# Sorted finish per tile, a split first load, and batch 0's norm and expert choice in the last scan step

## What is computed

```
h = einsum('bhid,oi,od->bho', x, weighted_sum, weight)
x = layernorm(h)
for _ in range(4):
    x = mamba_block(simple_rmsnorm(x), ...)   # in: conv (4 taps), silu, B, C, delta; 16 states per channel; out
h = h + x
z = layernorm(h)
expert = argmax(z @ W_router)                 # one of 4 for each token
y = gelu(z @ W1[expert] + b1[expert]) @ Wo + bo + z
h = h + layernorm(y) * gamma + beta
```

## Time and profile before

| | us |
|---|---|
| median of 3 runs (1889.51 to 1893.72) | 1891.31 |
| profiled execution | 1891.32 |
| its span, first to last instruction | 1889.2 |
| TensorE busy | 1782.5 (94%) |
| VectorE busy | 1552.8 (82%) |
| ScalarE busy | 1543.8 (82%) |
| GpSimd busy | 1510.4 (80%) |

### The profile page before, as it was taken

One profiled execution on the slowest core, in us unless ns is written; L12 is line 12 of the kernel. 1 busy time (PEld: TensorE's weight loads), 2 busy tenths in 40 slices (PEclk: granted clock), 3 DMA queues, 4 the chain that ended last, 5 costly groups with the idle time before them and its releaser, 6 DMA issues.

```text
span 1889.2 us, 31478 instructions
## 1 busy us (share of the span) xinstructions
PE 1782.5 (94%) x11920; PEld 1415.4 (75%) x11920; DVE 1552.8 (82%) x1707; ACT 1543.8 (82%) x2579; POOL 1510.4 (80%) x874
## 2 busy tenths in 40 slices
PE   6989899999999999999999999999999988789993
PEld 3447687878787878787878787878788777789993
DVE  1368989898989898989898989898989989853243
ACT  0269999999999999999999999999999987832230
POOL 0029999999999999999999999999999987631422
PEclk9999999999999999999999999999999989899997
DMA  7211111121212121211111111111111211163641
GB/s 272 99 68 45 58 47 68 44 71 40 74 38 76 37 71 44 71 44 67 48 62 52 59 56 57 58 54 61 50 65 46 80 57 68 38 250 129 231 143 59
DMA packets 46392, 144.24 MB, mean 76 GB/s; under 512 B 7009, under 2 KB 18529, under 8 KB 42914
## 3 DMA queue, kind: packets, MB, share of 16 engines
q1 hardware_dynamic: 41538, 114.97, 17.5%
q0 software_dynamic: 4704, 27.27, 4.0%
HBM read 119.67 MB, written 22.54 MB: 75 GB/s over the span
## 4 chain that ended last, share of the span: by engine, by line
PE 41%; ACT 24%; POOL 20%; DVE 8%; issue 6%; DMA 1%; SPq 0%; POOLq 0%; DVEq 0%; ACTq 0%
POOL hid L524 13%; ACT hid L709 12%; ACT dub_t L724 9%; PE b_ps L1469 8%; PE y_all L1482 7%; DVE hid L1141 6%; PE bank_a L1601 4%; POOL dub_t L515 4%; PE bank_b L1337 3%; PE y_all L1222 3%; PE bank_a L1337 2%; POOL du L505 2%; PE b_ps L1585 2%; PE y_all L1585 2%; PE bank_a L1346 2%
## 5 line engine op out<-in xcount | busy, mean ns | idle before, releaser
L1141 DVE TENSOR_TENSOR_SCAN hid<-hid,b_ps 128x512 f32<-128x512 f32 x1024 | 1199.2, 1206 | 102.0 <-PE b_ps L1469 89.6
L524 POOL TENSOR_TENSOR hid<-hid,c_rep 128x1024 f32<-128x1024 f32 x506 | 1191.8, 2390 | 97.7 <-DVE hid L1141 97.4
L1469 PEld LDWEIGHTS b_ps<-ident,dub_t 128*128 128x128 f32 x4096 | 486.4, 142 | 300.2 <-issue 180.5
L1469 PE MATMUL b_ps<-ident,dub_t 128*128 128x128 f32 x4096 | 630.7, 277 | 42.7 <-DVE hid L1141 40.4
L709 ACT ACTIVATE hid<-delta,neg_a 128x512 f32<-128x512 f32 x1024 | 659.6, 714 | 0.2
L1482 PE MATMUL y_all<-ident,hid 128*128 128x128 f32 x4096 | 620.5, 275 | 0.0
L724 ACT ACTIVATE dub_t<-du_t,b_t 128x512 f32<-128x512 f32 x784 | 505.2, 714 | 30.0 <-PE b_ps L1469 29.6
L1482 PEld LDWEIGHTS y_all<-ident,hid 128*128 128x128 f32 x4096 | 484.1, 142 | 2.9 <-POOL hid L524 2.7
L515 POOL TENSOR_SCALAR dub_t<-du_t,b_t 128x512 f32<-128x512 f32 x240 | 162.4, 702 | 0.0
L934 DVE SCALAR_TENSOR_TENSOR u<-bank_b,conv_w_sb,u 128x511 f32<-128x511 f32 (+2 forms) x192 | 139.6, 727 | 0.7
L1316 PE MATMUL bank_b<-xn,w_in_sb 128*128 128x512 f32 x256 | 129.9, 603 | 5.4 <-DVE u L934 3.9
(11 more groups left out here) (211 smaller groups left out, 1593.7 us busy)
## 6 DMA issues: line engine op xcount, KB each, us to landing
c_rep<-bc_dram SPq DMA_DIRECT2D x128, 512.0 KB, 3.7
hid<-x_t SPq DMA_DIRECT2D x4, 2048.0 KB, 8.5
xt<-x_dram SPq DMA_DIRECT2D x15, 512.0 KB, 3.4
x_dram<-x_out SPq DMA_DIRECT2D x15, 512.0 KB, 2.9
z_dram<-du SPq DMA_DIRECT2D x2, 1408.0 KB, 19.2
y_dram<-hid SPq DMA_DIRECT2D x22, 128.0 KB, 2.1
h_dram<-hid SPq DMA_DIRECT2D x4, 512.0 KB, 4.3
x_dram<-hid SPq DMA_DIRECT2D x3, 512.0 KB, 2.7
```

Of the source, the lines that this page charges most:

```text
L524: nc.gpsimd.tensor_tensor(part, part, c_rep[:, n % 2, s % GROUP, :].unsqueeze(1) .broadcast_to([P, HALF, SEQ]), ALU.mult).then_inc(hc_read ...
L1141: nc.vector.tensor_tensor_scan(hid[:, i % RING, d, :], hid[:, i % RING, d, :], b_ps[d % 2][:, :], 0.0, ALU.mult, ALU.add)\
L1469: last = nc.tensor.transpose(b_ps[d % 2][:, c * P:(c + 1) * P], dub_t[:, i % DUB, c, d * P:(d + 1) * P], ident[:, :])
```

## The change

It has four parts.

**Start.** The loads of `wd` and of batch 0's `x_t`, now in two halves, are issued from ScalarE's queue beside SyncE's; `wc` is made in two halves, and the token product waits for each half. The zeros for `z_dram` are no longer written at the start: `clear_rows` writes those of one pair in step 4 and of the other in step 6, together with zeros for `h2_dram` and padding ids for `id_dram`.

**Head of batches 0 and 1.** Epsilon and the scaling are GpSimd's (`head_root`); the statistics are spread over several slots. Batch 0's root and scaling move from step 14 to (15, 0), its turns to (15, 1) and (15, 2), the logits to (15, 3), the choice to (15, 4). `choose` reads the scores from PSUM and has seven instructions.

**Finish.** `h2` (the residual) and the token ids are scattered in the order of the tiles, as z is, and loaded back; z and h2 of a tile lie side by side in `z_part`. Each tile is then finished in its sorted order: `add_y` (y from PSUM plus z plus bias), `tile_moments`, `tail_root`, `tile_finish`, and an indirect transfer from GpSimd puts each row at its token's place in `out`, which has 22 x 128 more rows for the padding. `y_dram`, its stores and the gathers are gone. From tile 6 on the projections alternate between two banks.

**Order.** `rank(1)` and `lay_out(1)` come one tile earlier, `last_out` and the logits of batch 2 and 3 stand behind a projection instead of ahead of it.

```
+LATE = {6: (0, 1), 7: (2, 3), 8: (4,), 9: (5,), 10: (6,), 11: (7,), 12: (8, 9), 13: (10, 11)}
+FINISH_AT = [LATE.get(t, (t - 2,) if t > 13 else ()) for t in range(ALL_TILES)]
+MOMENTS_OF = [() if t in (0, LAY_T) else (t - 2, t - 1) if t == LAY_T + 1 else (t - 1,) for t in range(ALL_TILES)]
+ROOTS_AT = [{0: (), 1: (), 2: (0, 1), 5: (), 6: (4, 5)}.get(t, (t - 1,)) for t in range(ALL_TILES)]
...
+                    act.dma_start(hid[:, 0, :, :], x_t[0, :, 0:NI, :]).then_inc(x_first, 16)
+                    for d in range(TAPD):
+                        act.dma_start(wd[d::TAPD, :], w_t[d, :].partition_broadcast(P // TAPD)).then_inc(tw_in, 16)
+                    act.dma_start(hid[:, 1, :, :], x_t[0, :, NI:2 * NI, :]).then_inc(xT_in[0], 16)
...
+                    def clear_rows(g):
+                        sp.wait_ge(zero_made, 1)
+                        for rows, done in ((z_dram[g], z_zeroed), (h2_dram[g], h2_zeroed)):
+                            sp.dma_start(rows.rearrange("(j p) o -> p j o", p=P),
+                                         zero[:, :].unsqueeze(1).broadcast_to([P, TILES, D])).then_inc(done, 16)
+                        sp.wait_ge(ids_made, 2)
+                        sp.dma_start(id_dram[g].rearrange("(j p) o -> p j o", p=P),
+                                     pad_id[:, g * TILES:(g + 1) * TILES].unsqueeze(2), allow_slow_non_contiguous=True).then_inc(id_set, 16)
...
+                            if k in (4, 6) and g == 5:
+                                clear_rows((k - 4) // 2)
...
                     load_z(0)
                     store_x(STEPS - 2)
                     load_x_tokens(2)
-                    for p in range(3):
-                        store_y(p)
+                    load_h2(0)
+                    load_ids(0)
                     load_z(1)
...
+                    load_h2(1)
+                    load_ids(1)
...
                     def head_root(b):
+                        pool.wait_ge(bn_ready, 2 * TC * (b + 1))
+                        own = 2 if b == BATCH - 1 else 0
+                        nc.gpsimd.tensor_scalar(f_norm[:, own, :], moments[:, own, :, 1], 1e-5, None, ALU.add).then_inc(f_ve_ready, 1)
                         pool.wait_ge(f_ve_ready, b + 1)
-                        own = 2 if b == BATCH - 1 else 0
                         nc.gpsimd.tensor_tensor(f_norm[:, own, :], f_norm[:, own, :], half_power[:, :], ALU.pow).then_inc(f_root_ready, 1)
...
+                        for c in range(TC):
+                            nc.gpsimd.tensor_scalar(f_z[b][:, c, :], f_h2[b][:, c, :], moments[:, own, c, 0:1], f_norm[:, own, c:c + 1],
+                                                    ALU.subtract, ALU.mult).then_inc(z_ready, 1)
...
-                                if (k, s, half) == (STEPS - 2, 11, 1):
+                                if (k, s, half) == (STEPS - 1, 0, 1):
                                     head_root(0)
...
+                    for t in range(ALL_TILES):
+                        if t + WBUF < ALL_TILES:
+                            load_w1(t + WBUF)
...
+                        for n in ROOTS_AT[t]:
+                            tail_root(n)
...
+                        for n in FINISH_AT[t]:
+                            send_out(n)
+                    send_out(ALL_TILES - 2)
+                    tail_root(ALL_TILES - 1)
+                    send_out(ALL_TILES - 1)
...
-                    Z_T_COPY_AT = {(STEPS - 2, 15): (0, 0), (STEPS - 1, 0): (0, 1), (STEPS - 1, 9): (1, 1)}
+                    Z_T_COPY_AT = {(STEPS - 1, 1): (0, 0), (STEPS - 1, 2): (0, 1), (STEPS - 1, 9): (1, 1)}
...
+                        tt(o_row[:, t % O_RING, :], out_ps(t), z_rows(t)[:, 0:D], ALU.add).then_inc(y_added, 1)
...
-                    MOMENTS_AT = {(STEPS - 2, 11, 0): 0, (STEPS - 1, 5, 3): 1}
-                    SCALE_AT = {(STEPS - 2, 13, 0): 0, (STEPS - 1, 7, 0): 1}
-                    CHOOSE_AT = {(STEPS - 1, 2, 1): 0, (STEPS - 1, 9, 3): 1}
+                    STATS_AT = {(STEPS - 2, 10, 0): (0, 0), (STEPS - 2, 10, 1): (0, 1), (STEPS - 2, 11, 0): (0, 2), (STEPS - 2, 11, 1): (0, 3),
+                                (STEPS - 1, 4, 3): (1, 0), (STEPS - 1, 5, 0): (1, 1), (STEPS - 1, 5, 3): (1, 2), (STEPS - 1, 6, 0): (1, 3)}
+                    MEAN_AT = {(STEPS - 2, 11, 2): 0, (STEPS - 1, 6, 1): 1}
+                    CHOOSE_AT = {(STEPS - 1, 4, 0): 0, (STEPS - 1, 9, 3): 1}
...
-                            pe.wait_ge(y_kept, TURN_OF[t])
+                            pe.wait_ge(y_added, t - 1)
...
-                    Z_TURN_AT = {(STEPS - 2, 14, 0): (0, 0), (STEPS - 2, 15, 3): (0, 1), (STEPS - 1, 7, 3): (1, 0), (STEPS - 1, 8, 1): (1, 1)}
-                    LOGITS_AT = {(STEPS - 1, 0, 3): 0, (STEPS - 1, 9, 2): 1}
+                    Z_TURN_AT = {(STEPS - 1, 1, 2): (0, 0), (STEPS - 1, 2, 2): (0, 1), (STEPS - 1, 7, 3): (1, 0), (STEPS - 1, 8, 1): (1, 1)}
+                    LOGITS_AT = {(STEPS - 1, 3, 2): 0, (STEPS - 1, 9, 2): 1}
```

More of the change, by code:

```diff
@@ L298, in logits_ps, with out_ps, z_rows @@
                 return (bank_b[:, :] if b < 2 else y_ps[DC + b - 2])[:, 0:TC * EXPERTS]
+            def out_ps(t):
+                return (y_ps[DC + 1] if t >= BANKED and t % 2 else bank_a)[:, 0:D]
+            def z_rows(t):
+                return z_part[t // TILES][t % TILES // 4][:, t % TILES % 4, :]
             def rank_ps(g):
@@ L417, in store_out, with load_h2 @@
-                    def store_out(b):
-                        sp.wait_ge(res_ready, b + 1)
-                        sp.dma_start(out[b], y_tok[b]).then_inc(res_stored, 16)
+                            sp.dma_start(z_part[g][i][:, 0:n, 0:D], rows[:, 4 * i:4 * i + n, :]).then_inc(z_in[g][i], 16)
+                    def load_h2(g):
+                        sp.wait_ge(h2_out[g], 16 * CH)
+                        rows = h2_dram[g].rearrange("(j p) o -> p j o", p=P)
+                        for i in range(3):
+                            n = min(4, TILES - 4 * i)
+                            sp.dma_start(z_part[g][i][:, 0:n, D:2 * D], rows[:, 4 * i:4 * i + n, :]).then_inc(h2_in[g], 16)
@@ L901, in _ @@
                     dve.wait_ge(tw_in, 2 * TAPD * 16)
-                    nc.vector.tensor_tensor(wc, ws, wd.unsqueeze(1).broadcast_to([P, KT, D]), ALU.mult).then_inc(wc_ready, 1)
+                    for half in range(2):
+                        rows = slice(half * NI, (half + 1) * NI)
+                        nc.vector.tensor_tensor(wc[:, rows, :], ws[:, rows, :], wd.unsqueeze(1).broadcast_to([P, NI, D]), ALU.mult)\
+                            .then_inc(wc_ready, 1)
                     center(0)
@@ new lines, in tile_finish @@
+                    def tile_finish(t):
+                        o = t % O_RING
+                        dve.wait_ge(t_root_ready, t + 1)
+                        dve.wait_ge(centered, t + 1)
+                        if t % TILES == 0:
+                            dve.wait_ge(h2_in[t // TILES], 3 * 16)
+                        nc.vector.scalar_tensor_tensor(o_row[:, o, :], o_row[:, o, :], tile_norm[:, o:o + 1], z_rows(t)[:, D:2 * D],
+                                                       ALU.mult, ALU.add).then_inc(res_ready, 1)
```

395 lines of the change are left out of this document (208 added, 187 removed).

## The result

The changed kernel takes 1870.21 us (median of 4 runs, 1869.42 to 1873.22), the kernel before beside it 1892.37 us; the ratio is 0.9893 [0.988, 0.9905]. Forecast were 1854 us: 22 us came of the 37.7.

What follows compares the result with a forecast made beforehand. Four engines 94 to 99% busy bound inner steps, TensorE the tiles; 29.1 us without matmul followed. Terms -23.4 - 0.6 - 6.5 - 4.5 - 3.7 + 1.0 = -37.7 took 1891.3 to 1853.6 us, rounded to 1854; range 1845 to 1870.

Steps and rivals of the forecast that it cites:

- step 15: Last step before the tiles: work leaving VectorE and a better clock outweigh GpSimd's added scalings; -4.5 us, from 0 to -9.
- the end: After the last matmul: only one tile's chain is left, 5.7 us against 29.1; -23.4 us, no less than -20.
- the start: Before the first matmul: its 2.23 MB land sooner, so it starts near 11.2 instead of 14.9; -3.7 us, 0 to -6.
- rival (a): Last two steps give nothing, as VectorE's removed waits return as TensorE's waits for GpSimd's z; +11, 1865 us; chance 0.2.
- sign of being wrong: In step 15: z turns waiting for GpSimd's z by over 2 us would show the forecast wrong.
- +1.3: In step 15: cost of the first z turn waiting about 1.9 us for GpSimd's scaling; bounds +0.5 to +2.
- At most 9: Upper bound in us on the 5.7 us chain after the last matmul.
- Step 14: Second-last step: epsilon, scalings, two z turns and a slow clock go; -6.5 us, bounds 3.7 and 8.1.
- The cap: In step 14: a step with no extra work takes 95.0 us, which limits the gain to 7.0.
- The tile stage: Feed-forward tiles: TensorE's 177.4 us stay and a wait for a bank's copy goes; -0.6 us.
- The clears: Steps 4 and 6: doubled zero and id stores might delay the next c_rep load; +1.0 us, between 0 and +12.
- (d): Feed-forward tiles: GpSimd's queue becomes the bound; 1886 us, or 1927 with longer hold-ups; chance 0.04.

Runs made afterwards that it cites:

- forms: The changed kernel plus six groups of four GpSimd instructions, alone after the last store; 128x256 subtract and multiply took 1.22 us, multiply with one operand 0.47.
- split_form: The changed kernel with batch 0 scaled on ScalarE, batch 1 on GpSimd as multiply and add; 1865.6 us, ratio 0.9861.
- copy_early: The changed kernel with ScalarE's copy of batch 1's first turn one state earlier; 1883.1 us, ratio 0.9905, on a chip whose totals do not compare.
- unchanged: The changed kernel run once more without edits, as yardstick; 1871.3 us, ratio 0.9885.
- cheap_form: The changed kernel with both batches' scalings on GpSimd as multiply and add, and the small table loaded first at the start; 1870.0 us, ratio 0.9883.

## Why the prediction was wrong

The sum missed by 16.2 us: step 15 by 12.2, the end by 6.7, the start by 2.2, and the other terms gave 4.9 back.

**Step 15** is the step that failed, at "four scalings of 0.35 (half of 0.70 for 512 columns)". They take 1.22: 0.70 was a multiplication, and a subtraction on GpSimd costs 2.4 times as much (forms). Halving the columns was wrong too, but small. So the chain that TensorE's first z turn waits for was 4.84 us and not 1.4, and the turn waited 6.7 us and not 1.9, with a slow clock after it. The prediction had this path: rival (a), "a wait removed on VectorE comes back as TensorE's wait for GpSimd's z", and its sign of being wrong, such a wait of over 2 us. The sum has it at +1.3.

The price alone does not make up the miss. With the dear form gone for both batches (split_form) step 15 is 115.6, 3.1 to 5.3 us less and still 6.9 over the forecast's 108.7. What stood behind it is ScalarE's copy of batch 1's first turn. The prediction's remark on copies "one slot behind their turns" is on batch 0's at (15,1); batch 1's stands where it stood in the kernel before, its 1.1 us wait was in that trace, and no term has it. Taking it away gives 2.6 to 4.8 us alone (copy_early) and 4.8 on top of the cheap scalings (115.6 to 110.8). With both gone step 15 is 109.2 to 110.8; that this is near 108.7 is luck, as the forecast did not move that copy. A further slip: the 1.2 us of batch 0's two turns are taken off step 14 and added nowhere in step 15. And at that place in step 15 the scaling is no cheaper on VectorE, 5.17 us, since its SBUF instructions wait for GpSimd's.

By the Trainium skill, GPSIMD Engine Reference, Engine selection, GpSimd is some two times slower than VectorE for two-input elementwise work, and "1-input is roughly line-rate". The runs bear that out for multiply and add (0.47 to 0.55, where one scaling takes VectorE 0.40 when nothing holds it), and not for subtract (1.06 to 1.22).

**The end** was right as a chain (6.2 us for 5.7) and wrong as a sum. The term left out is GpSimd's close, 0.083 us for each indirect transfer of the program. The kernel before hid its 4.5 us behind the last store. The change adds 38 transfers (3.1 us) and puts GpSimd's last instruction at the very end, so 5.9 us of it stand bare. "At most 9" had no row for it.

**Step 14**: right within the code's own spread, -8.4 here and -5.5 in unchanged for -6.5. The cap does not hold: 92.5 us is below the 94.4 of an inner step, so the pattern is no floor; that this step does without some of its work may be why, and was not tried. The epsilon's share is bounded (2.7 to 5.6), that of scalings and turns was not tried alone.

**The start**: the terms were the bytes that the first matmul needs. What counts is all bytes on the rings beside them: in the changed kernel the second half of x and batch 1's x flow along, and the tables land at 12.0, later than in the kernel before (9.6). With those held back, the tables land at 9.2 to 9.4 and the first matmul comes at 10.5 to 10.6, where 11.2 was forecast and 13.3 measured. Then the clock before the first scan blurs it.

**The tile stage**: right, in this trace: 182.7 us from last scan to last matmul, as in every other run of this order but the two on the slower chip, which took 201.0. GpSimd is busy for 101.8 of 178 us and never late for TensorE, though it is nearer to it than the forecast lag of 10 us says: one changed order in the queues of VectorE and GpSimd exposed 7.1 us. **The clears**: nothing, for +1.0; the 4-byte rows kept SyncE 5.3 us in each of the two steps, with slack to spare.

**The chances** do not add up by themselves: (d) has 0.04 in the list and 0.02 + 0.03 in the split. Rival (a) comes closest to what happened: steps 14 and 15 together gave 0.7 us. Its 1865 and the 6.7 us that the end missed by give about 1871, where 1870.2 was measured.

## What to carry to other kernels

Cost a moved operation by a row with the same arithmetic, not only the same engine and shape; where none is there, the bound must be wide, and `a * x + b` is the form to move to GpSimd. When a producer is moved behind a consumer in an in-order queue, list every wait between the two: with two in a row, one fix alone can show nothing (cheap_form) or half (copy_early), and only both together show the whole gain. Have more than one trace of the same code before a difference of 2 us in a step is put down to an edit. Count the indirect transfers of the whole program when GpSimd works to the very end.
